# Attention over edges: shorter strips of zeros behind the gathers, and another order of steps

## The reference, cut to what matters

```python
h = relu(layernorm(x))
q, k, v = h @ Wq.T, h @ Wk.T, h @ Wv.T                  # [N, 8, 16] each
scores = einsum('ehc,ehc->eh', q[dst], k[src]) / 4 + edge_attr @ We.T
ex = exp(scores - segment_max(scores, dst)[dst])
x = x + segment_sum(v[src] * ex / segment_sum(ex, dst)[dst], dst)
h = relu(layernorm(x))
for layer in 3:                                        # each: (norm * (h @ W)[src]) summed by dst, then bias, relu, batch norm
    h = conv_and_norm(h)
x = x + h
```

## Time and profile before

| what | value |
|---|---|
| median of 3 runs | 6214.33 us |
| time of the profiled execution | 6205.67 us |
| its span | 6203.9 us |
| PE busy | 5259.4 us (85%) |
| DVE busy | 4526.3 us (73%) |
| ACT busy | 2295.7 us (37%) |
| POOL busy | 4496.4 us (72%) |
| granted clock of PE, mean | 0.766 of full speed |
| all strips of zeros (L734; L2070 and L2061) | 1413.0 us (723.2 in attention; 381.5 and 308.3 in aggregation) |

### The profile page before, as it was taken

How to read it: one execution, slowest core, us unless ns; L and a number is a source line. 1 busy time by engine, 2 the same in 40 slices (tenths; PEclk the granted TensorE clock), 3 DMA queues, 4 the chain that set the end, 5 groups by cost and what they waited for, 6 DMA issues and landing times. The chain is left out here.

```text
span 6203.9 us, 165021 instructions
## 1 busy us (share of the span) xinstructions
PE 5259.4 (85%) x49582; PEld 3541.0 (57%) x49582; DVE 4526.3 (73%) x13500; ACT 2295.7 (37%) x5686; POOL 4496.4 (72%) x6062
## 2 busy tenths in 40 slices
PE   3688888888888888874799699998899997699995
PEld 2355555555555555553577467675476765467674
DVE  7566666666666666668899688886488887788886
ACT  3333333333333333333344244443644443444442
POOL 2588888888888888867000198886298886588883
PEclk9655565555555655555677699999999999899997
DMA  4433333333333333324333443333433334533335
GB/s 134 137 100 99 100 99 99 99 99 100 99 98 100 99 99 99 99 80 134 110 92 95 122 117 112 112 117 99 136 113 114 114 112 106 179 112 114 114 111 163
DMA packets 542000, 688.39 MB, mean 111 GB/s; under 512 B 217072, under 2 KB 427905, under 8 KB 541722
## 3 DMA queue, kind: packets, MB, share of 16 engines
q0 software_dynamic: 140208, 338.71, 19.8%
q1 hardware_dynamic: 401692, 348.45, 18.8%
HBM read 619.25 MB, written 67.52 MB: 111 GB/s over the span
## 5 line engine op out<-in xcount | busy, mean ns | idle before, releaser
L730 POOL DMA_INDIRECT at_kv<-kv_tab,at_idx x1568 | 1541.5, 983 | 276.6 <-POOL at_rest L734 139.6
L2247 ACT ACTIVATE ag_msg<-ag_pair 128x768 bf16<-128x768 f32 x1200 | 944.2, 809 | 1371.1 <-PE ag_pair L2177 1298.5
L2186 PE MATMUL ag_sum<-ag_hot,ag_msg 128*128 128x240 bf16 x10800 | 1267.4, 267 | 1.1 <-DVE ag_msg L2116 0.7
L2186 PEld LDWEIGHTS ag_sum<-ag_hot,ag_msg 128*128 128x128 bf16 x10800 | 982.9, 98 | 334.0 <-issue 287.6
L2058 POOL DMA_INDIRECT ag_spill<-g_tab,ag_idx x600 | 587.2, 979 | 687.0 <-DMA ag_idx<-spill_tab 578.5
L2099 DVE TENSOR_SCALAR ag_hot<-iota_win,ag_node 128x240 bf16<-128x240 bf16 x4350 | 994.4, 339 | 0.0
L2067 POOL DMA_INDIRECT ag_spill<-g_tab,ag_idx x750 | 731.1, 975 | 126.3 <-POOL ag_rest L2070 80.9
L2177 PE MATMUL ag_pair<-xs,ag_pick 128*32 128x384 bf16 x14400 | 758.9, 330 | 67.3 <-issue 62.9
L734 POOL MEMSET at_rest<- 8x448 f32 x1568 | 723.2, 461 | 0.1
L2116 DVE CAST ag_msg<-ag_pair 128x768 bf16<-128x768 f32 x600 | 570.2, 950 | 131.5 <-PE ag_pair L2177 104.8
L2177 PEld LDWEIGHTS ag_pair<-xs,ag_pick 128*32 128x32 bf16 x14400 | 301.0, 96 | 330.0 <-issue 214.7
(11 more groups left out here) (333 smaller groups left out, 9313.9 us busy)
## 6 DMA issues: line engine op xcount, KB each, us to landing
ag_pick<-slot_tab SPq DMA_DIRECT2D x150, 768.0 KB
rk_hi_bc<-hi_tab SPq DMA_DIRECT2D x50, 896.0 KB
at_attr<-attr SPq DMA_DIRECT2D x196, 128.0 KB
at_qd<-q_tab SPq DMA_DIRECT2D x1568, 12.0 KB
at_kv<-kv_tab,at_idx POOLq DMA_INDIRECT x1568
ag_spill<-g_tab,ag_idx POOLq DMA_INDIRECT x1350
tr_dv<-dinv_tab SPq DMA_DIRECT2D x72, 256.0 KB
g_tab<-xs SPq DMA_DIRECT2D x48, 384.0 KB
```

The costliest lines, as they stand in the source:

```text
L730: nc.gpsimd.indirect_dma_start(kv[:, s.slot, ch, :], None, env["kv_tab"], bass.IndirectOffsetOnAxis(ap=idx[:, s.slot, ch:ch + 1], axis=0)) ...
L2186: last = nc.tensor.matmul(sum_ps[k][:, 0:WIN], row[:, part * DIM:(part + 1) * DIM], hot[:, k, ch, :], start=first and part == 0, stop=end ...
L2247: nc.scalar.activation(msg[:, p % 4, :, :], pair_ps[p % 3][:, :, 0:3 * DIM], ACT.Copy).then_inc(copied[p], 1)
```

## The change

`REST`, the length of each strip, goes from 448 to 320 in both stages. In attention the lists of DVE, PE and ACT are put in another order; `bias` runs for the block one later (lag 1 instead of 2) and waits for the scores of the block before and the `above` of two before; `spread_scale` writes into the bank ps_node, no longer ps_scale, and waits for the same two semaphores as `put_nodes` instead of the next block's `above`; `shrink` waits for `placed`. `fall_short` moves from the end of DVE's round to the next round (lag 4), for which `ml` has two buffers. POOL's and SP's lists are unchanged.

```diff
-REST = 448
+REST = 320
...
-        ml = tile("ml", [P, HEADS])
+        ml = tile("ml", [P, 2, HEADS])
...
-        sf_ps = ps_scale[:, 0:128]
+        sf_ps = ps_node[:, 144:272]
...
-        num_ps, den_ps = ps_node[:, 256:384], ps_node[AUXD:AUXROWS, 384:512]
+        num_ps, den_ps = ps_node[:, 272:400], ps_node[AUXD:AUXROWS, 0:128]
...
                 def add_bias(s):
...
+                    s.freed(dve, m_spread, 1)
...
                 def run_max(j):
...
-                        s.freed(dve, short_made, 1)
+                        s.freed(dve, short_made, 2)
...
                 def shrink(s):
-                    dve.wait_ge(scale_spread, s.nth)
+                    dve.wait_ge(placed, s.nth)
...
                 steps(dve, sh.BLOCKS, SLOTS, [
-                    (3, run_max(0)), (3, run_max(1)), (3, own_max), (2, products), (3, above_score),
-                    (4, scale_nodes), (4, load_bases), (3, node_max), (2, add_up), (3, load_first), (4, shrink),
-                    (3, raise_max), (2, add_bias), (4, merge), (0, place_one), (0, hot_one),
-                    (3, messages), (3, fall_short)], w)
+                    (2, products), (3, run_max(0)), (3, run_max(1)), (3, own_max), (4, fall_short), (2, add_up),
+                    (2, add_bias), (4, load_bases), (0, hot_one), (3, above_score), (4, scale_nodes), (3, node_max),
+                    (3, messages), (4, shrink), (4, merge), (0, place_one), (3, load_first), (3, raise_max)], w)
...
                 def spread_scale(s):
                     pe.wait_ge(scale_made, s.nth)
-                    pe.wait_ge(above_made, s.nth if isinstance(s.n, int) and s.n == sh.BLOCKS - 1 else s.nth + 1)
+                    pe.wait_ge(nodes_made, s.nth)
+                    pe.wait_ge(count_copied, s.nth)
...
                 def bias(s):
...
-                    s.freed(pe, above_made, 1)
-                    if not (isinstance(s.n, int) and s.n < 2):
-                        pe.wait_ge(scaled, 2 * (s.nth - 2))
+                    s.freed(pe, sc_made, 1)
+                    s.freed(pe, above_made, 2)
...
                 steps(pe, sh.BLOCKS, SLOTS, [
-                    (2, mask(0)), (2, mask(1)), (3, spread_max), (3, near_max), (4, spread_scale), (4, put_nodes),
-                    (3, turn_near), (1, spread_q), (2, bias), (3, turn_max), (2, turn_scores), (3, give_back),
-                    (2, spread_scores), (0, turn_hot), (0, turn_place), (3, sum_up)], w)
+                    (2, mask(0)), (2, mask(1)), (3, spread_max), (3, near_max), (2, turn_scores), (1, spread_q),
+                    (4, spread_scale), (4, put_nodes), (3, turn_near), (2, spread_scores), (1, bias), (3, sum_up),
+                    (0, turn_hot), (0, turn_place), (3, turn_max), (3, give_back)], w)
...
                 steps(act, sh.BLOCKS, SLOTS, [
-                    (3, exp), (4, copy_count), (3, scale_exp), (3, copy_max), (2, copy_scores), (0, cast_place),
-                    (3, gain_exp), (0, copy_hot), (0, copy_place), (0, widen_hot)], w)
+                    (4, gain_exp), (2, copy_scores), (3, exp), (4, copy_count), (0, widen_hot), (0, cast_place),
+                    (0, copy_hot), (0, copy_place), (3, copy_max), (3, scale_exp)], w)
```

More of the change, by code:

```diff
@@ L784, in run @@
                         dve.wait_ge(bc_made[j], s.nth)
-                        s.freed(dve, short_made, 1)
-                        nc.vector.tensor_reduce(ml[:, HALF * j:HALF * (j + 1)],
+                        s.freed(dve, short_made, 2)
+                        nc.vector.tensor_reduce(ml[:, s.slot % 2, HALF * j:HALF * (j + 1)],
                                                 ps_bc[j][:, :].rearrange("p (h e) -> p h e", e=P), AX.X, ALU.max
@@ L794, in own_max @@
                     s.freed(dve, near_made, 1)
-                    nc.vector.tensor_tensor(md[:, :, :], ml[:, :].unsqueeze(1).to_broadcast([P, C, HEADS]),
+                    nc.vector.tensor_tensor(md[:, :, :], ml[:, s.slot % 2, :].unsqueeze(1).to_broadcast([P, C, HEADS]),
                                             env["mask_c"][:, :].unsqueeze(2).to_broadcast([P, C, HEADS]), ALU.mult
@@ L843, in fall_short @@
                     s.freed(dve, less_made, 1)
-                    nc.vector.tensor_tensor(short[:, :], back_ps, ml[:, :], ALU.subtract).then_inc(short_made, 1)
+                    nc.vector.tensor_tensor(short[:, :], back_ps, ml[:, s.slot % 2, :], ALU.subtract).then_inc(short_made, 1)
                 def scale_nodes(s):
```

## The result

The changed kernel takes 7708.29 us (median of 4 runs, 7692.12 to 7718.44) against 6213.55: a ratio of **1.2407** (95% interval 1.2391 to 1.2422). The forecast was 6037 us.

A forecast was written before the change was run, and what follows sets the result against it. POOL was taken to bound attention, POOL and PE both to be full in aggregation. 6205.67 less 137 (attention) less 40 (aggregation) is 6028.7; with 8.7 for the median, 6037 us, range 5990 to 6150.

The forecast's parts named there:

- The strip's price: On POOL: a strip of 320 takes 354 ns, each gather comes 107 ns sooner, attention's round falls from 12.95 to 12.09 us.
- The failed step: On POOL in attention: shortening the strips makes no covered work come due, so the full 107 ns a gather is gained.
- the term of 2.50 us: Part of attention's chain: spread_scores, turn_hot and turn_place on PE and the step to ACT, 2.50 us together.
- The new order's chain: In attention, once around PE, ACT and DVE, closing through fall_short: 12.25 us a round, just above POOL's 12.09.
- spread_scale: On PE in attention: its new wait ends some 2.3 us after add_bias, when PE gets to it, so it costs nothing.
- shrink: On DVE in attention: waits for placed, 4.04 us into the chain; its loop was taken as shorter than the chain's.
- Aggregation: POOL's span falls from 14.93 to 13.97 us, PE becomes the bound at 14.64, and 150 spans save 40 us.
- Rival 1: In attention PE's clock rises above 0.59 and POOL's 12.09 us stays the bound: 6006 us, chance 0.22.
- Rival 2: On POOL in attention, closer gathers lengthen and give the saving back: 6174 us, chance 0.07.
- Rival 3: On DVE in attention, fall_short inherits the removed waits: 6109 us with one 0.37 us pause, 6182 with two; chance 0.12.
- Rival 4: On DVE in attention, the 1.2 us wait for gathers falls in series with the chain: 13.45 us a round, 6272 us, chance 0.07.
- the three signs: Wrong if attention's round stays at 12.9 us, gathers average over 1.08 us, or DVE's wait for gathers grows.

The follow-up runs named there:

- c1: The changed kernel (new order) with strips of 8 instead of 320: 6004 us, ratio 0.966 to the kernel before.
- e2: The kernel before with strips of 8 and bias issued one round ahead, with the changed kernel's waits and PSUM places: 6002 us, ratio 0.967.
- b3: The kernel before, old order, with strips of 8 instead of 448: 5751 us, ratio 0.926.
- b1: The kernel before, old order, with a strip of 320 and then one of 8 behind each gather: 6096 us, ratio 0.982.
- c2: The changed kernel (new order) with a strip of 320 and then one of 8 behind each gather: 6137 us, ratio 0.987 to the kernel before.
- d1: The kernel before, old order, with strips of 328 instead of 448: 7076 us, ratio 1.139.
- a1: The kernel before, old order, with strips of 320 in both stages: 7131 us, ratio 1.147.
- d2: The kernel before, old order, with strips of 352 instead of 448: 6991 us, ratio 1.125.
- a2: The changed kernel (new order) with strips of 448 again in both stages: 6218 us, ratio 1.000 to the kernel before.
- a3: The kernel before, old order, with strips of 320 in aggregation alone: 6706 us, ratio 1.080.
- d4: The kernel before, old order, with strips of 320 written on 128 partitions instead of 8: 6454 us, ratio 1.039.

## Why the prediction was wrong

- **The strip's price** (107 ns, POOL's round 12.09): right, 355 ns against 354. Its round was never reached.
- **The failed step** is the sentence "The strips hide no other work, so nothing that they covered comes due", and with it the chain's links from PE to another engine, taken at what they cost on time: 0.11 us to DVE, and the step to ACT inside the term of 2.50 us. With strips of 320 the step to ACT alone took 5.9 us in the round shown, and the round 18.3 us instead of 12.25. I had priced no update of PE that comes late. The hint was there, and I read past it: 0.14 of PE's recorded updates were already over 0.3 us late with 448, the worst by 2.5, in a kernel whose POOL bound hid it. Why the strip's length decides over it stays open.
- **The new order's chain** (12.25 us): right in size, 12.2 in c1, but in part by luck. In c1 the last links have some slack beside PE's own list, and e2 takes the same 12.2 without the chain through fall_short. I also held it against POOL's round alone and never worked out the *old* order's round, which can be at most 10.9 us (b3). By the forecast's own sum the old order, with strips of 320, would then have run at POOL's 12.09, so no part of the 137 us was the new order's to earn.
- **spread_scale** "costs nothing": in c1 PE has no wait before it, in e2 one of 0.3 us a round (36.3 us, 106 times). **shrink** as "the shorter loop" is doubtful: its wait for placed takes 1.4 us a round in c1 (151.2 us, 106 times) and 1.1 in e2.
- **Aggregation** (40 us): PE's updates came late there too (0.64 of them). Where none does (b3, 4100 to 4800 us), PE is full, as forecast, and the span is 700 x 9 / 423 = 14.89 us, not 14.64: PE's busy time filled the idle time that I had counted as the saving. That a shorter strip could just wait out the same DVE instruction didn't come true: L2061's strips went from 516 to 395 ns.
- **Rival 1**, the clock: no, 0.52. **Rival 2**, gathers that grow: not at 320 (958), but true in kernels without late updates, 1024 in b1 and 1039 in c2, where 8 x 0.055 = 0.44 us a round goes back of the 0.53 that c2's spacing saves. **Rival 3**, fall_short inherits the waits: the right place, priced at 0.37 us a pause; in the round shown the pause is 5.9. **Rival 4**, the slower case, had the sign and the wrong mechanism: DVE's wait for gathers fell to almost nothing (the products' group idles 18.3 us after the change, 144.1 in the earlier trace rows). None of the three signs that I had named for being wrong showed what came: the round didn't stay, the gathers didn't grow, and DVE's wait for them didn't either.
- By the Trainium skill ("SBUF — State Buffer", section "Who interferes with whom") only VectorE and GpSimd share a port and "PE and ACT never wait on anyone". The trace agrees as far as the products go (turn_place takes 0.31 us after the change and in c2). The page's rule is about ports and says nothing of when semaphore updates arrive, and those are what was late.

## What to carry to other kernels

A delay between transfers is a tuned constant, and its curve need not be smooth: here 256, 416 and none are clean, single strips of 288 to 384 on 8 partitions cost 8 to 18% with the old order, and the best value was nearly none or none, which only a sweep over the whole range finds. Before shortening what looks like padding, compare end of producer with start of consumer across engines; where the gap is many times its usual 0.1 us and the releaser "remote", look for late semaphore updates. And work out the chain of the present order as well as that of the new one, since today's bound can hide that the present order is already the better one.

## What the runs showed of the hardware

- While gathers follow each other behind single strips of 288 to 384 elements on 8 partitions, PE's semaphore updates come late (mean 1.1 to 1.3 us with the old order, up to 8.5), four of them 34 ns apart in the round shown, and at two moments in each gather's spacing, about half a spacing apart (in d1 0.5 to 0.7 and 1.2 to 1.4 us after a gather's start). DVE's and ACT's are on time (in the changed kernel, a1, d1 and d2 none is over 0.3 us late). SP is hit too: its register moves take 0.03 us, but of 862 in a1 from 1000 to 2300 us 40 took 0.3 to 0.72 us; in the kernels with late 0.00 none took over 0.1.
- Gathers mostly behave the other way: with single strips of 288 to 384 at most 3% of them take over 1.05 us, in the kernels with late 0.00 it is 6 to 13%. But c1 and e2 have neither (1%), and the kernel before, a2 and a3 have some of both (7 to 8%, and 0.13 to 0.14 late). Whether the two have a common cause, no run shows.
- Open: what in a strip puts the kernel in the one mode or the other. Not a limit on the spacing (1.495 late, 1.505 not, 1.526 late, 1.544 not), not a limit on the length (384 late, 416 not, 448 a little), and more bytes written don't end it (d4).
- Open too: whether the recording itself takes part in the delay. Each time here comes with a span and a granted clock that the profiler read, so no run tells what the kernels do without it.
